# A second layer norm taken tile by tile inside the attention, with its rows on GpSimd

## The reference, cut to what matters

```python
x = x + xattn(_layernorm(x), ctx_512, ...)       # 16 heads, softmax over 257 keys
hs_in = _layernorm(x)                            # (x - m) / sqrt(v + eps)
residual = hs_in
hs = _layernorm(hs_in, ln_w, ln_b)               # a norm of the norm, with weight and bias
mlp = gelu(hs @ fc1_w + fc1_b) @ fc2_w + fc2_b   # 512 -> 2048 -> 512
x = x + (mamba(hs) + mlp + residual)
```

## Time and profile before

| what | us |
|---|---|
| runs, median of 3 | 1071.37 |
| runs, lowest and highest | 1069.65, 1073.22 |
| the profiled execution's own time | 1073.56 |
| its span in the trace | 1071.7 |
| TensorE busy (share of the span) | 972.2 (91%) |
| VectorE busy | 566.9 (53%) |
| ScalarE busy | 413.5 (39%) |
| GpSimd busy | 416.1 (39%) |

### The profile page before, as it was taken

The page is one execution under the profiler, slowest core; times in us unless marked ns, Lnnn a source line. Parts: engine busy times, 40 slices in busy tenths (PEclk is TensorE's granted clock), DMA queues, the critical chain, the costliest instruction groups (busy, mean ns, idle before and its releaser), DMA issues. The chain is left out here.

```text
span 1071.7 us, 15903 instructions
## 1 busy us (share of the span) xinstructions
PE 972.2 (91%) x5479; PEld 815.3 (76%) x5479; DVE 566.9 (53%) x1067; ACT 413.5 (39%) x954; POOL 416.1 (39%) x444
## 2 busy tenths in 40 slices
PE   5898976899999983799999999899999999999988
PEld 4666645777777762688888898786778899999977
DVE  6233358888888837444554432324986433333335
ACT  2333347766676626423422224452333122222101
POOL 0787854333433306000000120405732879892041
PEclk9999988999999996899999999998999999999999
DMA  6776722111111102322241003412021856671143
GB/s 201 214 242 210 220 78 79 35 36 40 38 32 40 30 1 79 118 79 79 83 136 37 20 21 92 156 31 93 2 81 51 269 194 214 204 227 61 43 138 98
DMA packets 79001, 109.89 MB, mean 103 GB/s; under 512 B 14224, under 2 KB 46992, under 8 KB 78928
## 3 DMA queue, kind: packets, MB, share of 16 engines
q1 hardware_dynamic: 70320, 89.52, 26.6%
q10 hardware_dynamic: 6048, 11.01, 3.1%
q0 software_dynamic: 2560, 8.39, 2.4%
HBM read 83.13 MB, written 25.77 MB: 102 GB/s over the span
## 5 line engine op out<-in xcount | busy, mean ns | idle before, releaser
L43 PE MATMUL psum<-second_xT_hi,mlp_w_hi 128*128 128x512 f32 x272 | 108.1, 397 | 8.5 <-DVE mix_wo_lo L1556 5.7
L44 PE MATMUL psum<-second_xT_lo,mlp_w_hi 128*128 128x512 f32 x272 | 107.4, 395 | 0.0
L45 PE MATMUL psum<-second_xT_hi,mlp_w_lo 128*128 128x512 f32 x272 | 107.2, 394 | 0.0
L1070 POOL TENSOR_TENSOR all_x<-all_x,mlp_raw 128x512 f32<-128x512 f32 x8 | 10.0, 1291 | 185.4 <-DVE all_x L1568 185.4
L2081 ACT ACTIVATE moe_s<-psum 128x352 f32<-128x352 f32 x39 | 18.1, 465 | 156.6 <-PE psum L45 140.8
L43 PEld LDWEIGHTS psum<-second_xT_hi,mlp_w_hi 128*128 128x128 f32 x272 | 52.0, 191 | 20.9 <-DVE mix_wo_lo L1556 6.1
L2147 DVE TENSOR_TENSOR moe_hT_lo<-psum,moe_hT_hi 128x384 fp32r<-128x384 f32 x39 | 21.7, 558 | 83.0 <-ACT moe_hT_hi L2087 83.0
L1525 ACT ACTIVATE mlp_s<-psum,mlp_side 128x512 f32<-128x512 f32 x32 | 21.9, 683 | 110.1 <-PE psum L45 110.1
L1568 DVE TENSOR_TENSOR all_x<-all_x,psum 128x512 f32<-128x512 f32 x64 | 43.9, 687 | 33.1 <-PE psum L45 32.3
L43 PE MATMUL psum<-moe_w_hi,moe_tT_hi 128*128 x184 | 61.3, 333 | 0.0
L742 POOL TENSOR_TENSOR first_xT_hi<-q_rows,first_xT_hi 128x256 fp32r<-128x256 f32 x28 | 20.7, 739 | 104.4 <-ACT first_xT_hi L831 104.4
(11 more groups left out here) (326 smaller groups left out, 2926.5 us busy)
## 6 DMA issues: line engine op xcount, KB each, us to landing
mlp_raw<-in_fc SPq DMA_DIRECT2D x16, 512.0 KB, 4.8
kv_all<-all_x SPq DMA_DIRECT2D x28, 256.0 KB, 3.6
far_raw<-in_eg SPq DMA_DIRECT2D x10, 704.0 KB
far_raw<-in_eu SPq DMA_DIRECT2D x10, 704.0 KB
slot_rows<-mix_W SPq DMA_DIRECT2D x23, 256.0 KB, 5.8
slot_out<-far_rows ACTq DMA_DIRECT2D x23, 256.0 KB, 2.2
far_raw<-in_ed SPq DMA_DIRECT2D x10, 512.0 KB
far_rows<-slot_rows ACTq DMA_DIRECT2D x19, 256.0 KB, 2.7
```

Of the source, the lines that this page charges most:

```text
L43: e.matmul(out, hi_l, hi_r, start=first, stop=False)
L44: e.matmul(out, hi_l, lo_r, start=False, stop=False)
L45: return e.matmul(out, lo_l, hi_r, start=False, stop=last)
L1070: pool.tensor_tensor(g["x"][:, t, :], g["x"][:, t, :], b2, ALU.add).then_inc(x_plus, 1)
```

## The change

Seven of the eight tiles get their second norm inside the attention. A table gives the step at which each begins: `EARLY = (18, 20, 22, 24, 26, 30, 34)` for tiles 0 to 6. At such a step s VectorE aggregates the tile's statistics ahead of its maxima, and GpSimd takes the root and writes both normed copies itself (`norm.rows(pool, ...)`: two TENSOR_SCALAR of 128x512, subtract and multiply, with the mean and the factor as pointers). At s+1 TensorE transposes the second copy into a bank of scores ahead of the scores of that step, ScalarE scales it ahead of the exponentials and copies the high part at the end of its step, and GpSimd adds the first copy to x. At s+2 GpSimd subtracts the low part. Room for the columns and for the three scratch rows is found in queries of batches already done: so the batches are taken in natural order (0 first, where before the last four came first), the queries are stored in swapped halves (`place_of`), and the contexts are loaded in the matching order (`turn_of`). The weight and bias `wb` are loaded at the attention's start. Behind the barrier only tile 7 is normed, by VectorE as before; TensorE's first up matmul waits for the first weights alone (`w_ok` 1 in place of 2), its second half of columns for tile 7's low part, and its first down matmul for the second weights.

The core of the diff:

```diff
+EARLY = (18, 20, 22, 24, 26, 30, 34)
...
+    def aggregate(self, v, i):
+        t = self.first + i
+        v.bn_aggr(self.mv[:, t, :], self.g["stats"][:, t, :]).then_inc(self.aggr, 1)
+        v.wait_ge(self.aggr, i + 1)
+        v.tensor_scalar(self.var[:, t, 0:1], self.mv[:, t, 1:2], EPS, None, ALU.add).then_inc(self.var_done, 1)
+        v.tensor_scalar(self.var[:, t, 1:2], self.mv[:, t, 1:2], 1.0 + EPS, EPS * EPS, ALU.mult, ALU.add).then_inc(self.var_done, 1)
+
+    def root(self, pool, i):
+        t = self.first + i
+        pool.wait_ge(self.var_done, 2 * (i + 1))
+        pool.tensor_tensor(self.rstd[:, t, :], self.var[:, t, :], self.g["power"][:], ALU.pow).then_inc(self.rstd_done, 1)
+
+    def rows(self, v, i, r):
+        t = self.first + i
+        v.wait_ge(self.rstd_done, i + 1)
+        wait(v, self.x_added, i)
+        wait(v, self.transposed, i)
+        out, done = ((self.once, self.first_done), (self.twice, self.normed))[r]
+        v.tensor_scalar(out, self.g["x"][:, t, :], self.mv[:, t, 0:1], self.rstd[:, t, r:r + 1],
+                        ALU.subtract, ALU.mult).then_inc(done, 1)
...
+    def add(self, pool, i):
+        t = self.first + i
+        pool.wait_ge(self.first_done, i + 1)
+        pool.wait_ge(self.normed, i + 1)
+        pool.tensor_tensor(self.g["x"][:, t, :], self.g["x"][:, t, :], self.once, ALU.add).then_inc(self.x_added, 1)
+    def transpose(self, pe, i, bank):
+        pe.wait_ge(self.normed, i + 1)
+        for c in range(DC):
+            m = pe.transpose(self.g["psum"][:, bank, c * P:(c + 1) * P], self.twice[:, c * P:(c + 1) * P], self.g["ident"][:])
+        m.then_inc(self.transposed, 1)
...
+            for s in range(B + 2 + BPT):
+                if s in EARLY:
+                    norm.root(pool, EARLY.index(s))
+                    for i in range(2):
+                        norm.rows(pool, EARLY.index(s), i)
+                if s - 1 in EARLY:
+                    norm.add(pool, EARLY.index(s - 1))
+                if s - 2 in EARLY:
+                    norm.low_part(pool, EARLY.index(s - 2))
+                if s < B:
+                    rows_lo(s)
                 if s + 2 < B:
...
+                if s - 1 in EARLY:
+                    pe.wait_ge(exp_ok, NJ * min(s, B))
+                    norm.transpose(pe, EARLY.index(s - 1), scale_bank(s))
...
+                if s - 1 in EARLY:
+                    if s - 1 == EARLY[0]:
+                        act.wait_ge(wb_in, 16)
+                        act.wait_ge(q_ok, 20 + 1 - DONE)
+                    norm.scale(act, EARLY.index(s - 1), scale_bank(s))
...
+                if s - 1 in EARLY:
+                    norm.high_part(act, EARLY.index(s - 1))
...
+                if s in EARLY:
+                    v.wait_ge(stats_ok, EARLY.index(s) + 1)
+                    norm.aggregate(v, EARLY.index(s))
...
@@ -1502,7 +1560,8 @@
         @block.gpsimd
         def _(pool):
             after.gpsimd_first(pool)
-            norm.roots(pool)
+            norm.root(pool, 0)
+            norm.add(pool, 0)
             after.gpsimd(pool)
 
         @block.scalar
@@ -1537,8 +1596,9 @@
                 else:
                     after.scalar_first(act)
                 half_step(k, p, 1)
+            norm.scale(act, 0, BANK)
+            norm.high_part(act, 0)
             split(0, 0)
-            norm.high_parts(act)
             loop(act, group)
...
-            norm.statistics(v)
-            norm.normalise(v)
+            norm.aggregate(v, 0)
+            for i in range(2):
+                norm.rows(v, 0, i)
+            norm.low_part(v, 0)
             split(0, 0)
             loop(v, group)
             after.vector(v)
...
-                pe.wait_ge(w_ok, NWS * (k + 1))
+                pe.wait_ge(w_ok, 1 if is_first(k) else NWS * (k + 1))
                 for half in range(NHALF):
-                    if is_first(k):
-
-                        pe.wait_ge(norm.lo_done, TT // NHALF * (half + 1))
+                    if is_first(k) and half == NHALF - 1:
+                        pe.wait_ge(norm.lo_done, 1)
```

More of the change, by code:

```diff
@@ L751, in queries_lo @@
                 pool.wait_ge(q_hi_ok, b + 1 - DONE)
-                pool.tensor_tensor(q_lo[:, p, :], q[:, batch_of(b), :], q_hi[:, p, :].bitcast(F32), ALU.subtract).then_inc(q_ok, 1)
-            for s in range(B):
-                rows_lo(s)
+                pool.tensor_tensor(q_lo[:, p, :], q[:, place_of(b), :], q_hi[:, p, :].bitcast(F32), ALU.subtract).then_inc(q_ok, 1)
+            pool.memset(g["power"][:], -0.5).then_inc(power_set, 1)
+            pool.wait_ge(power_set, 1)
+            for s in range(B + 2 + BPT):
[9 more added lines that the diff above has]
+                    rows_lo(s)
                 if s + 2 < B:
@@ L1458, in phase_mlp @@
         U = MC * NHALF
-        norm = make_norm(n)
+        norm = AffineNorm(n, g, TT - 1, *norm_rows)
+        BANK = 7
         own = Parts()
@@ L1493, in _ @@
             load(0)
-            norm.load(sp)
             after.sync_first(sp)
@@ L2322, in build @@
         phase_context_tail(nc, d, g)
+        edge = ExitStack()
+        at_end = Names(nc, edge, "edge", side="right")
+        g["wb"], g["power"] = at_end.sb("wb", [P, 2, DC]), at_end.sb("power", [P, 2])
+        with ExitStack() as ctx:
+            xT2_hi, xT2_lo = second_columns(nc, ctx, "second")
         with ExitStack() as ctx:
             a = Names(nc, ctx, "q")
-            q = a.sb("q", [P, B, HS])
+            q = Names(nc, ctx, "queries", side="right").sb("q", [P, B, HS])
             G_hi, G_lo = a.sb("G_hi", [P, H * D], F32R), a.sb("G_lo", [P, H * D], F32R)
```

192 lines of the change are left out of this document (92 added, 100 removed).

## The result

The changed kernel takes **1062.43 us** (median of 4 runs, 1060.97 to 1063.09) beside 1072.3 for the kernel before: a ratio of 0.9883, 95% interval 0.9837 to 0.993. Timed twice more on other chips it gave 0.994 (0.99 to 0.998) and 0.9922 (0.99 to 0.9944). It is faster, by 6 to 12 us in the three timings and by some 8 by the steps of the traces.

A forecast was written before the change was run, and what follows sets the result against it. VectorE's step of 6.85 us was taken to set the attention's pace. Terms 32.4 + 1.8 + 4.6 + 1.5 - 20.1 gave +20.2 us, forecast 1092 us, range 1067 to 1106.

The forecast's parts named there:

- The join: Behind the attention: only one tile left to norm, so the first up matmul starts 20.1 us earlier.
- The weights' wait: At the first up matmul: moving the wait for the second weights costs nothing; without its cover, 1.2 us.
- The root: In the chain behind the barrier: a root of two elements a row takes 0.76 us.
- The duration of a row: GpSimd's TENSOR_SCALAR of 128x512 in the attention takes 2.55 us.
- the two passes: GpSimd's subtract and multiply counted as two passes, each like a TENSOR_TENSOR of 1.28 us, together 2.55.
- The hold: In the attention: VectorE's SBUF operations stand still while a GpSimd instruction on SBUF runs; basis of the 32.4 us.
- the adds: In the step after each tile's start, GpSimd's add to x holds VectorE: 0.3 us a tile, 1.8.
- The walk: Step 20 followed operation by operation: 12.3 us for 6.85, so 5.4 more a step, 32.4 for six tiles.
- Tile 6: End of the attention, without cover: TensorE stands 4.2 us for the rows, plus 0.4 of transposes: 4.6.
- The load: Ahead of tile 0's rows: the ISA row before GpSimd's new operation costs 1.5 us, once.
- Rival 1: GpSimd's rows at the copy's rate, 0.6 us: 1062 us, faster; below 1.3 us an instruction the change wins; chance 0.10.
- Rival 3: GpSimd's TENSOR_SCALAR doesn't hold VectorE; the cost is TensorE's wait for rows, about 1.4 a step: 1069 us; chance 0.08.

The follow-up runs named there:

- e7_forms: Changed kernel with other forms of GpSimd's row operation in tiles 1 to 4 (one or two operations, pointers or constants, copy); one trace, batch 17 to 31 111.03 us.
- e13_low_by_vector: e8_spare_row with tile 4's low part in step 28 taken by VectorE in place of GpSimd; 1053.68 us, ratio to before 0.9865.
- e4_two_tensors: Changed kernel with each normed row of the seven tiles written by two TENSOR_TENSOR of GpSimd in place of one TENSOR_SCALAR; 1069.62 us, ratio to before 1.0005.
- e9_copies: Changed kernel with GpSimd's rows of tiles 0 to 6 written as plain copies of x; one trace, batch 17 to 31 111.89 us, last stretch 34.01.
- e10_no_add: Changed kernel with GpSimd's add to x of tiles 0 to 6 shrunk to one column; one trace, batch 17 to 31 108.17 us for 108.25.
- e6_pool_order: Changed kernel with GpSimd's list reordered (root, low part, second row, old low parts, first row) and tile 6's rows by VectorE; 1060.69 us beside 1067.43, ratio to before 0.9871.
- e8_spare_row: e6_pool_order with the three scratch rows dealt out anew among the same spent queries; ratio to before 0.9893, batch 17 to 31 106.22 us.
- after_again: The changed kernel run again, unchanged, beside other runs on one chip; ratio to before 0.994, batch 31 to the join 39.21 us.
- e2_second_first: Changed kernel with GpSimd writing the second normed row ahead of the first; 1058.76 us, ratio to before 0.9907.

## Why the prediction was wrong

**The join: right.** 20.1 us said, 20.4 measured, each link within 0.3. The weights' wait: 1.2 said, 1.13 measured once its cover was taken away. The root: 0.76 said, 0.73.

**The duration of a row: mis-sized.** 2.55 us said, 2.08 measured, and for another reason than the two passes: in e7_forms the first operation costs 1.5 us and a second adds 0.4 to 0.5. The Trainium skill, GPSIMD Engine Reference, "Elementwise — side-by-side cycle accounting", whose rule would put it near the copy, doesn't fit either: the copy takes 0.6, the TENSOR_SCALAR of two operations 2.08, and even that of one operation 1.5.

**The hold: the step that failed.** The prediction put it so: "while a GpSimd instruction on SBUF runs, VectorE's L885, L891 and L896 stand still". All rows behind it were of operations that read two tensors. On it stood 32.4 us for the rows and low parts of tiles 0 to 5 and 1.8 for the adds; the six tiles cost 6.8 in all. Beside GpSimd's TENSOR_SCALAR the same three take 0.24, 0.16 and 0.69 in step 18, and are held in no step longer than to 0.6 us behind its start; beside TENSOR_TENSOR they are held as said. The Trainium skill, SBUF — State Buffer, "Who interferes with whom", has a VectorE instruction of two SBUF inputs contend with a GpSimd instruction that reads SBUF, over an exclusive lock that the first to issue gets for the whole instruction; the second 0.69 of L952 (281.06) within the 4.45 us of L218 is against that for TENSOR_SCALAR, and e13_low_by_vector and e4_two_tensors agree with it for TENSOR_TENSOR.

**The walk: wrong by itself too.** With rows by two tensors its premise holds, and tiles 0 to 5 still cost 14.1 us, not 34. It let every hold add up; in the traces a hold costs what the held operation is ahead of. Where it falls on the tiny operation behind the first maximum, the step is longer by about its whole 1.1 us (1.10 in step 28; 0.8 to 1.3 in six steps of e9_copies). On the second of the two large operations it costs too (step 30 of e9_copies, 1.03). On L947 it costs nothing while ScalarE is late (e10_no_add). On the first of the two large operations (L955 in e9_copies, 1.46 us at 296.32) it cost nothing either: that step took 6.86 us. VectorE otherwise waits 0.42 there for `context_hi`, and the tiny operation behind it, 0.44 in the earlier trace rows, took 0.18.

**What stands in its place, 6.8 us for six tiles.** Statistics ahead of the maxima, 0.33 a tile: 2.0. Step 28's hold: 1.1, by the timeline. Step 19, 1.6 beyond the statistics: e6_pool_order took 0.4 of it away, and e8_spare_row 1.3 more by ending ScalarE's wait for `queries_lo`. The other 2.1 us stand in the steps 21, 23, 25 and 27 (0.54, 0.31, 0.66, 0.60), in which the scaling waits for L247. In e8_spare_row, where no scaling waits for GpSimd, nothing of these is left (-0.3 in the four). That kernel's order differs in more than this wait, so that the 2.1 are put down to it by their place and not by an edit of it alone. In the new order the steps 20, 22, 24 and 26 are longer instead (0.47, 0.23, 0.46, 0.21): there L247 holds the tiny operation behind the second maximum, which takes 0.88 or 0.65 us for 0.17. No run tested this. The prediction said of ScalarE only that the 2.1 us of a tile fit into its wait for the maxima; that the scaling's own wait stood in front of the exponentials was not in it.

**Tile 6: right in place, low.** 4.6 said, 5.2 measured, and 6.7 in after_again: the wait was 3.22, not 4.2, and the half-speed stretch behind it, left out, costs 1.5 to 3 us by its length. That the sum came near in the first trace is two errors against each other. **The load: too high,** 1.5 said, nothing seen: the rows of tile 0 start as soon behind the root as those of later tiles, 0.11 and 0.10 us. The figure of some 6 us that the Trainium skill gives (GPSIMD Engine Reference, "Instruction dispatch") is not seen either.

**The rivals.** Rival 1 has the measured number, 1062, by luck: it has the rows at 0.6 us, and they take 2.08. Its limit of 1.3 us a row, below which alone the change would be faster, is wrong too. Rival 3, a TENSOR_SCALAR that doesn't hold VectorE, was the right mechanism and had a chance of 0.08; its 1069 put the cost on TensorE's wait for the rows, 1.4 a step, which e2_second_first showed to cost nothing; the 6.8 us came from elsewhere.

## What to carry to other kernels

A hold seen between two engines belongs to the forms of operation that were seen in it; before it is multiplied over a new form, give the case that the new form doesn't do it the weight of an unknown. Price a hold or a wait by what stands behind the held operation, not by its length: the same 1.2 us cost 1.1, or nothing, by which tiny operation it fell on, and shortening GpSimd's work made the steps longer by moving its adds onto the wrong ones. Where work is put into a loop's slack, follow the in-order list of each engine that touches it: here the added scaling waited for a third engine, and all exponentials with it.

## What the hardware showed that was not expected

- GpSimd's TENSOR_SCALAR of 128x512 takes 1.5 us for one operation and 1.9 to 2.1 for two, more than a TENSOR_TENSOR of that size (1.28, or 1.04 where the second tensor is read with a stride of zero) and 2.5 to 3.5 times a copy (0.6).
- It is the only one of the three that keeps VectorE's SBUF operations waiting for a part of its time alone: to 0.6 us behind its start, of 2.08. Beside a copy L944 took 0.61 us (279.82, the copy from 279.80).
- The hold works both ways: GpSimd's operation took 1.49 us for 1.04 behind VectorE's L963, which itself took 1.23 for 0.69 behind GpSimd's operation before. A duration read beside the other engine is no measure of an operation: the second row of tile 0 took 2.36 us for 2.08 by it.
- Steps repeat to 0.03 us between executions at the same clock, while the parts around them move by 5 to 20 us; one step at a granted clock of 0.78 cost 1.1 us.
